# Local attention: VectorE divides the outputs in front of the sums of squares instead of behind them

## What is computed

```python
def attn_layer(x, Wqkv, qs, ksc, Wo):          # 16 heads of 64, windows of 32 tokens
    q, k, v = split_heads(x @ Wqkv)
    q = l2norm(q) * qs
    k = l2norm(k) * ksc                        # l2norm: t / sqrt(sum of squares)
    q = q * cos * scale + rotate_half(q) * sin * scale
    k = k * cos / scale + rotate_half(k) * sin / scale
    out = local_attention(q, k, v)             # softmax over own and previous window, times v
    return out @ Wo

for i in range(6):
    x = attn_layer(shift_tokens(x), Wqkv[i], q_scale[i], k_scale[i], Wo[i]) + x
    x = ffn_layer(shift_tokens(x), ln_g[i], ln_b[i], W1[i], b1[i], W2[i], b2[i]) + x
```

## Time and profile before

| what | us |
|---|---|
| median of 3 runs | 3852.21 (3849.74 to 3853.78) |
| the profiled execution, whole | 3852.91 |
| its span | 3851.1 |
| TensorE busy | 3664.3 (95%) |
| VectorE busy | 3136.7 (81%) |
| ScalarE busy | 2882.2 (75%) |
| GpSimd busy | 2450.8 (64%) |
| mean granted TensorE clock | 0.98 of full |
| sums of squares (L1046), 384 of them | 449.3 (1170 ns each) |
| outputs times reciprocals (L1098), 384 of them | 261.6 (681 ns each) |

### The profile page before, as it was taken

How to read it: one execution, slowest core, us unless ns; L and a number is a source line. 1 busy time by engine, 2 the same in 40 slices (tenths; PEclk the granted TensorE clock), 3 DMA queues, 4 the chain that set the end, 5 groups by cost and what they waited for, 6 DMA issues and landing times. The chain is left out here.

```text
span 3851.1 us, 189308 instructions
## 1 busy us (share of the span) xinstructions
PE 3664.3 (95%) x70910; PEld 2934.8 (76%) x70910; DVE 3136.7 (81%) x9407; ACT 2882.2 (75%) x8517; POOL 2450.8 (64%) x2556
## 2 busy tenths in 40 slices
PE   7869999999999999999999999999999999899998
PEld 4558888688886788876888868888678887466666
DVE  7878888688887788877888878888788887576766
ACT  5758888478885688865888848888578885577776
POOL 3657777377774677755777647777377773455543
PEclk8979999999999999999999999999999999999999
DMA  1013333233332233332333323333233332100000
GB/s 48 1 55 82 81 81 82 59 82 81 81 81 72 70 81 82 81 85 56 82 81 81 82 60 80 81 81 83 58 85 80 82 81 53 41 1 0 0 1 23
DMA packets 305294, 246.06 MB, mean 64 GB/s; under 512 B 74485, under 2 KB 299860, under 8 KB 304340
## 3 DMA queue, kind: packets, MB, share of 16 engines
q1 hardware_dynamic: 305108, 243.72, 25.1%
HBM read 24.54 MB, written 2.12 MB: 7 GB/s over the span
## 5 line engine op out<-in xcount | busy, mean ns | idle before, releaser
L1236 POOL TENSOR_TENSOR wa_t<-wa_t,wa_rn 128x512 f32<-128x512 f32 x768 | 785.2, 1043 | 281.3 <-DVE wa_rn L1064 278.6
L896 ACT ACTIVATE wa_pb<-wa_sc,wa_nm 128x64 f32<-128x64 f32 x3072 | 670.1, 329 | 368.3 <-DVE wa_nm L1086 340.4
L1242 POOL TENSOR_TENSOR wa_t<-wa_t 128x512 f32<-128x512 f32 x384 | 496.3, 1292 | 408.4 <-DVE wa_t L1040 408.4
L1038 DVE TENSOR_TENSOR wa_t<-wa_pj,wa_ctab 128x512 f32<-128x512 f32 x768 | 528.0, 687 | 209.7 <-PE wa_ta L640 165.1
L45 PE MATMUL wa_pj<-lw_wqkv_high,wa_xhigh 128*128 128x512 f32 x1152 | 533.5, 463 | 36.5 <-DVE wa_t L1040 18.2
L879 ACT ACTIVATE wa_sq<-wa_pj 128x512 f32<-128x512 f32 x768 | 487.0, 636 | 61.4 <-PE wa_pj L47 59.9
L1251 POOL TENSOR_TENSOR wa_t<-wa_t 128x512 f32<-128x512 f32 x384 | 490.0, 1276 | 0.0
L47 PE MATMUL wa_pj<-lw_wqkv_high,wa_xlow 128*128 128x512 f32 x1152 | 461.2, 400 | 0.0
L46 PE MATMUL wa_pj<-lw_wqkv_low,wa_xhigh 128*128 128x512 f32 x1152 | 457.8, 397 | 0.4 <-issue 0.4
L1046 DVE TENSOR_REDUCE wa_raw<-wa_sq 128x16 f32<-128x1024 f32 x384 | 449.3, 1170 | 0.0
L699 PE MATMUL wa_ob<-wa_oT,lw_wo 128*128 128x128 f32 x3120 | 418.4, 277 | 2.1 <-DVE wa_on L1098 1.9
(11 more groups left out here) (310 smaller groups left out, 8613.8 us busy)
## 6 DMA issues: line engine op xcount, KB each, us to landing
wa_vv<-wa_vt SPq DMA_DIRECT2D x2304, 65.0 KB
wa_vv<-wa_vt SPq DMA_DIRECT2D x1152, 32.5 KB
lw_wqkv<-L_ffn_Wqkv SPq DMA_DIRECT2D x6, 1536.0 KB, 6.2
lw_xs<-yT SPq DMA_DIRECT2D x96, 64.0 KB
lw_fs<-yT SPq DMA_DIRECT2D x48, 128.0 KB
lw_xs<-yT SPq DMA_DIRECT2D x96, 63.8 KB
lw_fs<-yT SPq DMA_DIRECT2D x96, 63.8 KB
lw_wo<-L_ffn_Wo SPq DMA_DIRECT2D x6, 512.0 KB, 4.2
```

Of the source, the lines that this page charges most:

```text
L896: last = nc.scalar.activation(pb[:, u.par(2), p, e, :], SC[:, e, p * KEYS:(p + 1) * KEYS], ACT.Exp, bias=nm[:, u.par(2), e, p:p + 1])
L1038: nc.vector.tensor_tensor(t1[:, b, j], x, table(ctab, slice(0, HD)), ALU.mult)
L1236: nc.gpsimd.tensor_tensor(here, here, rn[:, u.par(1), j * HG:(j + 1) * HG].unsqueeze(2).broadcast_to((128, HG, HD)), ALU.mult).then_inc(s. ...
L1242: nc.gpsimd.tensor_tensor(t1[:, b, 0], t1[:, b, 0], t2[:, b, 0], ALU.add).then_inc(s.qadd_done, 1)
```

## The change

In VectorE's `slot` the call of `sums(u)` moves from in front of the outputs to behind them. The reciprocals, the outputs, the sums and the clamp stay as they are, with the same waits.

```diff
                     if u.has(3):
                         dve.wait_ge(s.pv_done, u.count(1, 3, 1))
                         nc.vector.reciprocal(rs[:, :, :], ov[:, :, :, HD]).then_inc(s.rs_done, 1)
-                    if u.has(0):
-                        sums(u)
                     if u.has(3):
                         dve.wait_ge(s.rs_done, u.count(1, 3, 1))
                         if u.was(5):
@@ -1098,6 +1096,8 @@
                         nc.vector.tensor_tensor(on[:, u.par(3)].rearrange("p a e d -> p e a d"), ov[:, :, :, 0:HD],
                                                 rs[:, :, :].unsqueeze(3).broadcast_to((128, 2, PR, HD)),
                                                 ALU.mult).then_inc(s.norm_done, 1)
+                    if u.has(0):
+                        sums(u)
                     if u.has(0):
                         clamp(u)
```

## The result

The changed kernel takes 3968.15 us (median of 4, 3964.36 to 3973.11), the one before 3851.6 in the same comparison. The ratio is 1.0303, with a 95% interval of 1.0291 to 1.0315: slower by 3.0%, 117 us. The forecast was 3989 us, in a range of 3895 to 4035.

A forecast was written before the change was run, and what follows sets the result against it. TensorE was taken to set the attention slot at 6.60 us; a loop through late squares makes it 6.98. 360 slots x 0.38 = 137 us on the median 3852.21 gives 3989 us, range 3895 to 4035.

The forecast's parts named there:

- The step that carried it: Attention slots: sums start 0.71 us later, 0.31 covered by the exponentials, 0.40 reaches ScalarE's squares; the slot grows 0.38 us.
- The three terms of the loop: Attention slot: reciprocals to squares 2.05, squares to mask 3.03, mask to next reciprocals 1.90; 6.98 us against 6.60.
- The first term: Reciprocals to squares: 0.84 us until the sums start, 1.17 for the sums, 0.04 to reach ScalarE; 2.05 us.
- The last: Mask matmuls to the next slot's reciprocals, through the value products on TensorE: 1.90 us, taken from a late slot.
- The base of 6.60: Length in us of an attention slot before the change, set by TensorE; chosen between 6.575 and 6.65.
- Absorption: Rival for the attention slots: sums still end early enough, TensorE stays full, no change, 3852 us; chance 0.10.
- only VectorE's chain binds: Rival: value products are not in the loop; VectorE's chain of 6.88 us sets the slot, 101 us more, 3953; chance 0.22.
- The clock: Rival: TensorE idles 5% of each slot and its clock falls, 120 us on top, 4110; chance 0.03.
- The extra run on VectorE: VectorE from reciprocals to clamp grows from 1.81 to 2.04 us; the 0.23 us lies within its idle 0.43.
- The outputs' earlier end: VectorE's outputs finish about 0.97 us sooner; TensorE gains at most 1.9 us in the whole run, counted as nothing.
- TensorE busy some 6.6 of 7.0 us: Sign in the attention slots: TensorE no longer always busy, idle in front of the weight transposes and values projection.
- the time of 3950 us: By the skill's rule, outputs start 0.13 us behind the reciprocals, the slot is 0.11 us shorter than forecast, near 3950 us.

The follow-up runs named there:

- The run with the pause: Two idle copies on ScalarE in front of the first squares of every unit from the fifth on, in the kernel before: 3912.2 us, 1.0180.
- the run with two buffers: Changed kernel with two buffers for the squares, so ScalarE's squares wait for the sums two units back: 3872.5 us, ratio to the kernel before 1.0060.
- eight units: Changed kernel with two buffers for the squares and VectorE's loop written out for eight units instead of four: 3857.6 us, 1.0023.

## Why the prediction was right

The step that carried it held. The sums move by 0.71 us and more; the exponentials cover 0.31 us of it, the rest reaches the squares, and most of that reaches the slot. The run with the pause shows the same with VectorE's order untouched, and the run with two buffers takes 2.4 of the 3.0% back.

The three terms of the loop, as predicted and as the slot above has them: reciprocals to squares 2.05, measured 1543.10 - 1540.93 = 2.17; squares to mask 3.03, measured 2.98; mask to reciprocals 1.90, measured 1547.96 - 1546.08 = 1.88 here, and 1540.93 - 1539.23 = 1.70 in the slot in front. On the mean of the six layers' inner slots they are 2.14, 2.99 and 1.79. The predicted 6.98 us stand against 6.92 to 6.93 measured, and 360 x 0.38 = 137 us against 117 to 120. The forecast was 21 us too high. Two errors in opposite directions lie in it. The first term was too small: the outputs start 0.24 to 0.33 us behind the reciprocals, and the sums take 1209 ns instead of 1168. The kernel before could have told the first of these: at the end of a layer, where no sums stand in between, its reciprocals start at 1193.60 and its outputs at 1193.93, 0.33 us apart. The last was too large: I took it from one slot with late squares, whose reciprocals wait for the value products, while in the new state they stand right behind the maxima in many slots (0.61 us, at 1540.93) and wait in others (0.79, at 1547.96). The base of 6.60 is the measured mean. (439.00 - 418.74) / 63 = 0.32 us more per slot is a direct measure of what I put at 0.38.

The rivals. Absorption is refuted by the squares at +2.31. That only VectorE's chain binds is refuted by the run without the Newton step; the two loops are within about 0.1 us of each other, so its time of 3953 us was near, nearer to the measured 3968 than the forecast of 3989. It is the runs and not the time that decide between the two. The clock did not fall: it is 1.00 in the slots and 0.98 in the mean, as before.

The extra run on VectorE was mis-sized too: from reciprocals to clamp it is 2.14 us on the mean, 0.33 more than the 1.81, and not 0.23 more. That it cost nothing held for the changed kernel only, where the squares are later still. I had compared it with a mean idle time of 0.43 us. It does not fit into the slot with the branch, and that is most of the 24 us that remain when the squares no longer hide it. The 0.43 us were not all of VectorE's idle time either, as the prediction has it: 26.30 - 23.46 = 2.84 us in four slots are 0.71 in each, of which 0.43 stand in front of the rotation.

The outputs' earlier end gained nothing: TensorE's wait for them went from 1.9 us to 2.7. Of the signs, "TensorE busy some 6.6 of 7.0 us" was off: the view shows 27.25 of 27.71, 6.81 of 6.93. Busy time went up by 77 us on the page with the same instructions, and only 43 of the 120 us are seen as idle: the single matmuls add up to 31 us more, and they overlap less on the profile where they wait.

The Trainium skill, "VectorE: DVE Perf Modes", section "The DRAIN you can't avoid", has the rule that a semaphore between two operations costs nothing extra. Here the dependent outputs start 0.24 to 0.33 us behind the reciprocals, where the independent sums stood 0.13 behind them. So the rule does not hold here, and the time of 3950 us that it gave was 18 too low.

## What to carry to other kernels

An operation that frees a buffer for another engine has a due time; moving it is free up to that engine's own arrival. Beyond that, where the bound engine waits behind the freed buffer, most of it is lost: here 0.18 us of 0.24, and 0.32 of 0.47. Follow the loop round: who waits for the freed buffer, what is queued behind that wait, and when it comes back to the first engine. And compare an extra tenth of a microsecond on an engine with its idle time in each slot of a loop, the one with the branch above all, not with the mean.

## What had not been expected of the hardware

The sums take 1.17 us behind the reciprocals and 1.21 us behind the outputs; their mean went from 1170 to 1209 ns with the same operands. Behind the maxima, in the run that moved them the other way, they take 1.21 us too. The outputs went from 681 ns behind the sums to 692 behind the reciprocals.

VectorE's branch back to the loop's start costs it about 0.4 us between two operations (0.68 instead of 0.25 from start to start with two buffers; 0.66 instead of 0.29 with eight units). The kernel before hides that entirely, as writing the loop out there changes nothing. Writing it out in the changed kernel gained 0.5 us per saved branch. Of these, 0.43 show as shorter slots, but only 0.09 in the gap at the branch itself.
